# Graph attention and neighbour layer on one core: adjacency tiles turned in pairs, and value parts packed in 132-byte rows

## What is computed

```python
# layer 0: graph attention, 8 heads of 64 units
feats = einsum('bnf,hfu->bhnu', x, W)
e_self, e_neigh = feats . a_self, feats . a_neigh
dense = leaky_relu(e_self[..., :, None] + e_neigh[..., None, :], 0.2) + NEG_BIG * (1 - A)
out = einsum('bhij,bhju->bhiu', softmax(dense), feats) + b
x1 = layernorm(x + relu(concat_heads(out)))
# layer 1: mean over neighbours
agg = einsum('bij,bjf->bif', adj, x1) / deg
y = layernorm(x1 + relu(concat([x1, agg]) @ W1.T))
```

## Time and profile before

| what | value |
|---|---|
| runs | 3599.88, 3609.08, 3612.85 us |
| profiled execution | 3602.66 us (span 3600.9, mean granted clock 0.974) |
| TensorE matmul busy | 3413.5 us (95%) |
| TensorE weight load busy | 2912.9 us (81%) |
| VectorE busy | 2467.0 us (69%) |
| ScalarE busy | 1738.2 us (48%) |
| GpSimd busy | 285.0 us (8%) |
| DMA | 248.58 MB, mean 69 GB/s |

### The profile page before, as it was taken

How to read it: one execution, slowest core, us unless ns; L and a number is a source line. 1 busy time by engine, 2 the same in 40 slices (tenths; PEclk the granted TensorE clock), 3 DMA queues, 4 the chain that set the end, 5 groups by cost and what they waited for, 6 DMA issues and landing times.

```text
span 3600.9 us, 136785 instructions
## 1 busy us (share of the span) xinstructions
PE 3413.5 (95%) x59456; PEld 2912.9 (81%) x59456; DVE 2467.0 (69%) x4364; ACT 1738.2 (48%) x2185; POOL 285.0 (8%) x253
## 2 busy tenths in 40 slices
PE   6998989989899998999989899898998989989998
PEld 5978879787796877969779697886977869788795
DVE  5857668576685756858578485774857758576685
ACT  2635436364363644626346273462735527355363
POOL 0010100101001010100101001010010100101001
PEclk9999999999999999999999999999999999999999
DMA  5113031120312203122031220312203131130310
GB/s 170 59 38 108 26 113 57 51 99 23 116 51 60 96 18 122 45 76 81 20 125 39 77 79 25 125 33 89 68 27 123 33 98 59 38 118 27 94 33 24
DMA packets 98408, 248.58 MB, mean 69 GB/s; under 512 B 14720, under 2 KB 14720, under 8 KB 97792
## 3 DMA queue, kind: packets, MB, share of 16 engines
q1 hardware_dynamic: 97792, 239.38, 20.6%
HBM read 205.26 MB, written 34.08 MB: 66 GB/s over the span
## 4 chain that ended last, share of the span: by engine, by line
PE 94%; issue 3%; DVE 2%; ACT 1%; DMA 0%; SPq 0%; POOL 0%; ACTq 0%; DVEq 0%; POOLq 0%
PE six L843 77%; PE pair L843 12%; PE six L988 2%; PE pair L872 1%; PE pair L881 1%; PE six L872 1%; PE six L881 1%; DVE trl L600 0%; DVE stats L786 0%; ACT mask L414 0%; DVE adj_t L605 0%; DVE s_bc L783 0%; PE six L909 0%; DVE mask L797 0%; DVE mask L544 0%
## 5 line engine op out<-in xcount | busy, mean ns | idle before, releaser
L843 PE MATMUL six<-x_parts,mask 128*128 128x65 bf16 x16384 | 1550.7, 193 | 1.0 <-issue 0.9
L843 PE MATMUL six<-third,mask 128*128 128x65 bf16 x16384 | 1550.4, 193 | 0.6 <-issue 0.2
L843 PE MATMUL six<-rest,mask 128*128 128x65 bf16 x16384 | 1550.6, 194 | 0.0
L843 PEld LDWEIGHTS six<-x_parts,mask 128*128 128x128 fp8e4 x16384 | 1537.5, 97 | 5.7 <-issue 4.9
L843 PEld LDWEIGHTS six<-third,mask 128*128 128x128 fp8e4 x16384 | 1536.4, 97 | 0.6 <-issue 0.6
L843 PEld LDWEIGHTS six<-rest,mask 128*128 128x128 fp8e4 x16384 | 1533.9, 97 | 3.2 <-issue 1.4
L441 ACT ACTIVATE step<-s_bc,n_step 128x1024 uint16<-128x1024 f32 x1024 | 1094.2, 1138 | 382.8 <-DVE mask L671 382.0
L671 DVE TENSOR_TENSOR mask<-adj_t,step 128x1024 uint16<-128x1024 uint16 x1024 | 651.3, 685 | 24.5 <-ACT step L441 22.6
L843 PE MATMUL six<-adj_t,x_parts 128*128 128x512 fp8e4 x1536 | 388.5, 380 | 2.7 <-ACT x_parts L463 1.5
L392 POOL TENSOR_TENSOR s_bc<-feat,rden 128x512 f32<-128x512 f32 x112 | 124.0, 1112 | 3071.8 <-DVE s_bc L714 3043.0
L843 PEld LDWEIGHTS six<-adj_t,x_parts 128*128 128x128 f16 x1536 | 146.4, 98 | 179.3 <-issue 18.3
(11 more groups left out here) (118 smaller groups left out, 4830.5 us busy)
## 6 DMA issues: line engine op xcount, KB each, us to landing
adj_nat<-in_adj_dram SPq DMA_DIRECT2D x128, 512.0 KB, 4.7
s_bc<-self_scores SPq DMA_DIRECT2D x128, 512.0 KB, 3.7
xs<-in_x_dram SPq DMA_DIRECT2D x128, 256.0 KB, 2.8
out_dram<-mask SPq DMA_DIRECT2D x128, 256.0 KB, 3.0
adj_nat<-in_x_dram SPq DMA_DIRECT2D x64, 256.0 KB, 3.4
step<-in_x_dram SPq DMA_DIRECT2D x64, 256.0 KB, 3.5
xs<-in_L_gnn_W_dram SPq DMA_DIRECT2D x1, 2048.0 KB, 11.9
feat<-in_L_gnn_W_dram SPq DMA_DIRECT2D x4, 256.0 KB, 4.3
```

What stands on the lines that cost most here:

```text
L843: return pe.matmul(o, l, r, start=start, stop=stop, skip_group_check=True)
```

## The change

Five things are changed.

1. All 8 adjacency tiles of graph b+1 are turned in graph b: two behind each of tiles 4, 5 and 6, tiles 6 and 7 behind the last product. VectorE copies two of them in each of `ln1(5)`, `ln1(6)`, `ln1(7)`, and 6 and 7 behind. The late loads are issued earlier in the SP queue. Before the loop all 8 tiles of graph 0 are turned.
2. The three value parts of both sets are bfloat16 tensors of their own, in the space of the x1 parts, with 66 elements (132 bytes) to a row. `val32` is one fp32 scratch for all heads.
3. The making of the parts becomes a relay: VectorE makes the fp32 value in the scratch (`value_whole`), ScalarE copies it to the first part (`part_of(0, ..)`), VectorE subtracts that in place (`value_rest`), ScalarE copies the second part (`part_of(1, ..)`), VectorE makes the third (`value_last`).
4. Places: on VectorE, `value_whole` of head h+1 stands after mask 8h + 7, `value_rest` after the next head's mask 0, `value_last` after its mask 2. On ScalarE the two copies stand after steps 3 and 4 of the head itself. The halves of head 0: the first before step 0 and mask 0, the second after steps 3 and 4, between masks 1 and 4.
5. The sums of head h-1 are taken after mask 8h + 7 (groups 0 and 1), and group 2 after mask 0 of the head behind; those of head 6 after the last mask. GpSimd's second low part of x1 waits for the end of the attention.

```diff
+        U2 = U1 + 1
+        PART = 2 * T * U2
+        pool16 = x1_parts[:, :, :, :].rearrange("p k t d -> p (k t d)").bitcast(BF16)
+        def parts_at(first):
+            rows_of = pool16[:, first:first + PARTS * PART].rearrange("p (s k t u) -> p s k t u", s=PARTS, k=2, t=T)
+            return [rows_of[:, i, :, :, 0:U1] for i in range(PARTS)]
+        val = [parts_at(0), parts_at(2 * T * D - PARTS * PART)]
+        val32 = sb("val32", [P, 2, T, U1], F32)
+        lower = sb("lower", [P, T, U1], F32)
...
@@ sync
                 for t in range(T):
+                    for late in {4: (3, 4), 5: (5, 6), 6: (7,)}.get(t, ()):
+                        load_late_adj(b + 1, late)
                     sp.wait_ge(res_ok.sem, res_ok.at(b, t + 1))
                     load_x(b + 1, t)
                     if t >= 2:
                         store_y(b, t - 2)
-                    if t >= 4:
-                        load_late_adj(b + 1, t - 1)
...
-                load_late_adj(b + 1, T - 1)
@@ gpsimd, x1_low
+                    if t == 1:
+                        pool.wait_ge(sums_ps.sem, sums_ps.at(b, H * GROUPS))
@@ scalar
+                def part_of(i, h, tiles=slice(0, T)):
+                    before, done = ((val_f32, val_p0), (val_rest, val_p1))[i]
+                    act.wait_ge(before.sem, before.at(b, 1 if tiles.stop == HALF else h + 2))
+                    copy(val[h % 2][i][:, :, tiles], val32[:, :, tiles]).then_inc(done.sem, 1)
...
+                part_of(0, 0, FIRST)
                 weight_exp(qry_exp[:], ts_hi, SLOPE - 1.0)
+                part_of(1, 0, FIRST)
                 for g in range(H * T):
                     make_step(g)
+                    h, jt = divmod(g, T)
+                    if jt in (3, 4):
+                        part_of(jt - 3, h, slice(0, T) if h else SECOND)
@@ vector
+            def value_whole(b, h, tiles=slice(0, T)):
+                n = tiles.stop - tiles.start
                 if h >= 2:
                     dve.wait_ge(sums_ps.sem, sums_ps.at(b, (h - 1) * GROUPS))
+                if h >= 1:
+                    dve.wait_ge(val_p2.sem, val_p2.at(b, h + 1))
+                dve.tensor_tensor(val32[:, :, tiles], feat[...], key_w[...], ALU.mult).then_inc(val_f32.sem, 1)
+            def value_rest(b, h, tiles=slice(0, T)):
+                dve.wait_ge(val_p0.sem, val_p0.at(b, value_count(h, tiles)))
+                dve.tensor_tensor(val32[:, :, tiles], val32[:, :, tiles], val[h % 2][0][:, :, tiles],
+                                  ALU.subtract).then_inc(val_rest.sem, 1)
+            def value_last(b, h, tiles=slice(0, T)):
+                dve.wait_ge(val_p1.sem, val_p1.at(b, value_count(h, tiles)))
+                dve.tensor_tensor(val[h % 2][2][:, :, tiles], val32[:, :, tiles], val[h % 2][1][:, :, tiles],
+                                  ALU.subtract).then_inc(val_p2.sem, 1)
...
                 feature_rows(b, 5)
-                adj_rows(b, 6)
...
-                value_parts(b, 0, FIRST)
-                adj_rows(b, 7)
+                value_whole(b, 0, FIRST)
+                value_rest(b, 0, FIRST)
+                value_last(b, 0, FIRST)
...
                 feature_rows(b, 7)
+                dve.wait_ge(ft_sb.sem, ft_sb.at(b, T))
+                value_whole(b, 0, SECOND)
                 mask_word(2)
+                value_rest(b, 0, SECOND)
                 mask_word(3)
-                dve.wait_ge(ft_sb.sem, ft_sb.at(b, T))
-                value_parts(b, 0, SECOND)
+                value_last(b, 0, SECOND)
                 mask_word(4)
...
-                    if jt == 3 and h >= 1:
+                    if jt == T - 1 and h < H - 1:
+                        value_whole(b, h + 1)
                         if h == 1:
                             dve.wait_ge(qry_ok.sem, qry_ok.at(b, 1))
-                        head_sums(b, h - 1, 0, 2)
-                        head_sums(b, h - 1, 2, 3)
-                    if jt == (4 if h else 6) and h < H - 1:
-                        value_parts(b, h + 1)
+                        if h >= 1:
+                            head_sums(b, h - 1, 0, 2)
+                    if jt == 0 and h >= 1:
+                        value_rest(b, h)
+                        if h >= 2:
+                            head_sums(b, h - 2, 2, 3)
+                    if jt == 2 and h >= 1:
+                        value_last(b, h)
+                head_sums(b, H - 2, 0, 2)
+                head_sums(b, H - 2, 2, 3)
...
                     if more and t >= HALF + 1:
                         x_low(b + 1, t - 1)
-                        adj_rows(b + 1, t - HALF - 1)
+                        adj_rows(b + 1, 2 * (t - HALF - 1))
+                        adj_rows(b + 1, 2 * (t - HALF - 1) + 1)
...
                 if more:
-                    adj_rows(b + 1, 3)
+                    adj_rows(b + 1, 6)
+                    adj_rows(b + 1, 7)
                 ln1_end(T - 1)
-                if more:
-                    adj_rows(b + 1, 4)
-                    adj_rows(b + 1, 5)
@@ tensor
                 features(b, 5)
-                turn_adj(b, 6)
-                turn_adj(b, 7)
...
+                pe.wait_ge(head_ok.sem, head_ok.at(b, (H - 1) * GROUPS))
                 if more:
                     scores(b + 1, 0)
...
-                    if more and t >= HALF:
-                        turn_adj(b + 1, t - HALF)
+                    if more and HALF <= t < T - 1:
+                        turn_adj(b + 1, 2 * (t - HALF))
+                        turn_adj(b + 1, 2 * (t - HALF) + 1)
...
                 if more:
-                    turn_adj(b + 1, 4)
-                    turn_adj(b + 1, 5)
+                    turn_adj(b + 1, 6)
+                    turn_adj(b + 1, 7)
```

More of the change, by code:

```diff
@@ L128, in gat_sage_kernel @@
         mask = sb("mask", [P, MASK_SLOTS, N], U16)
[L129 to L135, removed]
         sc_nat = sb("sc_nat", [P, T, SC], F32)
@@ L219, in gat_sage_kernel @@
         val_f32 = signal("val_f32", H + 1)
+        val_p0 = signal("val_p0", H + 1)
+        val_p1 = signal("val_p1", H + 1)
         val_rest = signal("val_rest", H + 1)
@@ L557, in _, with value_count @@
                                   ALU.subtract).then_inc(w1_lo, 1)
-            def value_parts(b, h, tiles=slice(0, T)):
-                count = 1 if tiles.stop == HALF else h + 2
+            def value_count(h, tiles):
+                return 1 if tiles.stop == HALF else h + 2
+            def value_whole(b, h, tiles=slice(0, T)):
                 n = tiles.stop - tiles.start
-                first, second, last = (part[:, :, tiles] for part in val[h % 2])
-                whole, rest = val32[h % 2][:, :, tiles], rest32[h % 2][:, :, tiles]
                 if h >= 2:
                     dve.wait_ge(sums_ps.sem, sums_ps.at(b, (h - 1) * GROUPS))
-                dve.tensor_tensor(whole, feat[:, tiles, h, :].unsqueeze(1).broadcast_to([P, 2, n, U1]),
+                if h >= 1:
+                    dve.wait_ge(val_p2.sem, val_p2.at(b, h + 1))
+                dve.tensor_tensor(val32[:, :, tiles], feat[:, tiles, h, :].unsqueeze(1).broadcast_to([P, 2, n, U1]),
                                   key_w[:, :, tiles, h:h + 1].to_broadcast([P, 2, n, U1]),
                                   ALU.mult).then_inc(val_f32.sem, 1)
[L570 to L573, removed]
+            def value_rest(b, h, tiles=slice(0, T)):
[6 more added lines that the diff above has]
+                                  ALU.subtract).then_inc(val_p2.sem, 1)
             def head_sums(b, h, k0, k1):
@@ L833, in _ @@
                 x_low(0, t)
-            for t in range(6):
+            for t in range(T):
                 adj_rows(0, t)
```

## The result

The kernel after took 3667.48 us (median of 4 runs, 3662.41 to 3674.98) against 3604.48 us (median of 4, 3598.98 to 3612.85) for the kernel before beside it: ratio 1.0174, 95% interval 1.0145 to 1.0204. It is slower by 63 us. The profiled execution took 3666.84 us (span 3664.7, mean granted clock 0.976).

A forecast was written before the change was run, and what follows sets the result against it. TensorE was taken to bound the kernel (94% of the chain). The terms -39 + 6 + 2 + 78 + 22 - 66 + 2 = +5 on the profiled 3602.66 us gave 3608, written as 3610 us; range 3560 to 3680.

The forecast's parts named there:

- rival (a): Attention matmuls: stride is not the cause, packed rows stay at 31.3 ns, the 66 us are missing, 3676 us; chance 0.25.
- Boundary, -39: At each graph's end, tiles turned in pairs: branch 2.15 us sooner, taken as 2.6 us, 15 times: -39 us.
- The 5 us of issue stay: At the loop's branch between graphs: TensorE's 5 us stretch of issue remains, and so does the half clock behind it.
- Start of the attention, +6: First key tile of each graph: the relay of head 0's parts starts it 0.4 us later, 16 times, +6 us.
- The mask of key tile 4: In head 0 of the attention: this mask comes 0.15 us late, +2 us.
- Head 1, +78: Start of head 1: TensorE waits 4.9 us for VectorE's third part, 16 times, +78 us.
- Half clock behind it, +22: Behind head 1's wait: the clock falls to 0.50, adding 1.4 us a graph, +22 us.
- Rival (b): Head 1's wait costs less: clock stays up (3588 us), or most of the 78 us vanish (3510 to 3560); chance 0.17.
- The lead then grows: From head 2 on: parts ready at 29.3, wanted at 30; ScalarE needs 10.5 us a head, TensorE 12.
- Packed rows, -66: Attention matmuls outside head 0: packed moving rows cut the spacing from 31.3 to 29.8 ns, -66 us (bounds 0 and -85).

The follow-up runs named there:

- adj_only: The kernel before with only the adjacency part of the change (turns, copies, late loads moved): 3546.27 us, 0.9811 of the kernel before.
- dve_heads01: The changed kernel, but VectorE alone makes all parts of heads 0 and 1, the relay starting at head 2: 3632.67 us, 1.0061 of the kernel before.
- early_copies: The changed kernel with head 1's five relay steps moved earlier on VectorE and ScalarE: 3640.66 us, 1.0096 of the kernel before.
- experiments 9 to 12: Changed kernel with head 1's parts earlier (3640.66 us), also scratch last (3612.62), adjacency part alone repeated (3545.91), then head 2's parts earlier too (3568.60).
- strided: The changed kernel, but the first two parts lie in every second bfloat16, as before: 3717.45 us, 1.0289 of the kernel before.
- scratch_last: The changed kernel with the fp32 scratch and the sums' buffer declared behind all other tensors: 3644.99 us, 1.0108 of the kernel before.
- early_two: early_last with head 2's parts made earlier in the same way: 3568.60 us, 0.9885 of the kernel before.
- parts_only: The changed kernel with its adjacency part undone: 3730.72 us, 1.0319 of the kernel before.
- early_last: early_copies with the scratch and lower also declared behind all other tensors: 3612.62 us, 1.0016 of the kernel before.

## Why the prediction was right and where it was wrong

The forecast was 3610 us and "same", with 3560 to 3680 as range; 3667 lies inside the range, in the "slower" that had 0.42, and near the time of rival (a), but not by its mechanism. That the range held it is luck in part: its upper half stood for rows that gain no pace, and they gained it. In the order of its steps:

- **Boundary, -39: too small.** The adjacency wait went as foreseen; `adj_only` measures the whole part at -60 to -66 us. Per graph it is 5.3 us less between last product and R and 1.3 more among the products, for the three turns that now stand there (1.25 in `adj_only`): 4.0 where I had 2.6. Up to the release the step was right: counted from the last product's start, TensorE is released at 5.9 us before (the adjacency copy) and at 2.4 after (the sum), 3.5 sooner, less 1.3 for the turns: the 2.15 that I had. The step that failed is "The 5 us of issue stay". Before, the last turn and 5.0 us of issue (4.0 to 6.3) stand whole behind the release. After, both turns are made while TensorE waits for the sum, and only 3.9 to 4.4 us lie between the sum (1417.22) and R (1421.08). The row of 71.1 us of issue after has 5.1 us each time, but part of that runs beside the wait.
- **Start of the attention, +6: right** (+0.3 us a graph against +0.4). The mask of key tile 4 comes 0.09 us late (I had 0.15), but key tile 2 waits 0.24 us for its mask too, in every graph, which I did not have; with one stop more in the last graph head 0 loses 7 us where I had 2.
- **Head 1, +78: right** in place, mechanism and size: 15 stops of 4.7 us and one of 2.6. `dve_heads01` and `early_copies` show that the relay's late places make it; in both, VectorE's operations stand earlier as well, so the share of ScalarE's copies alone is not measured. **Half clock behind it, +22: right**, 24 us measured. Rival (b) falls with that.
- **"The lead then grows": right only because of the stop.** With the stop at head 1 cut short, heads 2 and 3 waited in turn (experiments 9 to 12).
- **Packed rows, -66: this term failed.** The mechanism holds: stride sets the pace (`strided`), against rival (a). But the pace fell by 1.14 ns, not 1.5 (my product with 1.5 makes 65 us; the 66 come of the unrounded 1.54), so -56 us over all eight heads; and some 46 us of that came back as stops for instructions (beyond the matmuls' own pace, 51.7 us in heads 2 to 7 after, 5.4 before). Net about -10. I had treated the distance of starts as the only limit of TensorE; the next one, how fast its instructions come, stood just under it. The landings of the instruction queue show that the stops end with them; no kernel here changed the supply itself. Not all of the 46 us are owed to the pace: the adjacency part alone, at 31.4 ns, has 21 to 24 us of such stops where the kernel before has 6.
- **Not in my list: the products of layer 1.** 18 us for a moved address (22 in all with what `scratch_last` wins in the attention), which no step of mine looked at.

By terms, then: boundary -60, start +5, wait at head 1 +76, half clock +24, pace -56, stops +46, head 0 +7, products +18 and ahead of the loop +5 give +65, against +63 measured. My sum had +5. The two large errors against me (packed rows -10 in place of -66, and the addresses' 18 us) were partly covered by the boundary's 21 in my favour.

The Trainium skill (SBUF — State Buffer, Specifications) would have packed rows gain nothing, since strided ones already have more than two hits in a 16-byte line. The runs do not agree: 31.46 against 30.16 ns a matmul, and 41 to 50 us of the whole. That it came near the net result is chance.

The best version measured is the adjacency part alone (3546, 1.8% under before). Packed parts with early relays and the scratch at the end take 3569 with the adjacency part: they are not worth having on top of it.

## What to carry to other kernels

A change of two halves can hide a gain behind a loss: run each half alone first. A copy handed to a half-idle engine is late where that engine has no lead yet, which is at the start of a stage, and curing the first late place uncovers the next; look at its lead at each hand-over, not at its busy share. When a stream of small matmuls gets faster, ask what feeds it, its instructions too; and declare a new tensor behind the old ones, or check the pace of untouched matmuls afterwards.

## What the runs showed of the hardware that was not expected

- **Addresses alone move the pace of 512-column fp32 products**: 228 ns became 234 when everything from feat on moved by 6240 bytes, in both kernels and in both directions. Which pair of addresses collides was not found.
- **A dense stream of matmuls and weight loads can outrun its instructions.** It stops at multiples of about 125 matmuls (up to 2.0 us) and goes on 1.2 to 1.9 us after a 16 KB piece of the instruction queue has landed. In heads 2 to 7 that made 6 to 24 us a run at 31.3 to 31.5 ns a matmul, and 31 to 68 us at 30.1 to 30.4 ns (31 in `early_two`, 68 in `parts_only`), so kernels of one pace differ widely too.
- **Every second bfloat16 as moving operand costs 4%** at 65 columns (31.46 against 30.16 ns), and rows of 130 instead of 132 bytes 1% (30.42).
- **Stops of 1.6 us at head 1 left the granted clock up, stops of 4.7 us there were followed by matmuls at half of it each time** (96 matmuls in 3.06 and 4.59 us). **Those between cost the clock in some graphs only**: stops of 1.9 to 2.5 us at head 2 in 4 of 16 (`early_last`) and 10 of 16 (`early_copies`), stops of 2.6 us in head 0 in 9 of 16 (`dve_heads01`). In which graphs it falls stays open.
